# Loading two tiles ahead in the weight dequantisation of a two-layer macaron transformer

## The reference

```python
# layer 0
x = x + 0.5 * L0_ffn(layernorm(x))        # ternary weights, 1024 -> 4096 -> 1024
x = x + L0_attn(layernorm(x))             # linear attention, then an FFN with GELU inside it
x = x + 0.5 * L0_ffn(layernorm(x))
# layer 1
x = x + 0.5 * L1_ffn(x)                   # int weights, used twice
x = x + L1_attn(x)                        # softmax attention, 16 heads of 64
x = x + 0.5 * L1_ffn(x)

def _dequant(q, scales, g):               # q: int32 0..255, g = 128
    w = (q.astype(jnp.float32) - 128.0).reshape(K // g, g, N) * scales[:, None, :]
    return w.reshape(K, N)                # fc1: 1024 x 4096, fc2: 4096 x 1024
```

## Time and profile before

| | us |
|---|---|
| median of the runs (2) | 15,925.6 (15,891.4 to 15,959.7) |
| the profiled execution | 15,981.4 |
| its span on the slowest core (core 6) | 15,979.8 |
| spans of the 8 cores | 15,761.4 to 15,979.8 |
| TensorE busy | 9,455.1 (59%) |
| VectorE busy | 3,824.6 (24%) |
| ScalarE busy | 3,534.6 (22%) |
| GpSimd busy | 417.6 (3%) |

### The profile page before, as it was taken

How to read it: one execution, slowest core, us unless ns; L and a number is a source line. 1 busy time by engine, 2 the same in 40 slices (tenths; PEclk the granted TensorE clock), 3 DMA queues, 4 the chain that set the end, 5 groups by cost and what they waited for, 6 DMA issues and landing times.

```text
span 15979.8 us, 134598 instructions; the slowest of 8 cores (15761.4 to 15979.8 us)
## 1 busy us (share of the span) xinstructions
PE 9455.1 (59%) x37062; PEld 4058.4 (25%) x37544; DVE 3824.6 (24%) x7679; ACT 3534.6 (22%) x6356; POOL 417.6 (3%) x781
## 2 busy tenths in 40 slices
PE   0018884233333566553088878874777767677877
PEld 0003332111111344442033333332111111112333
DVE  0111214332233211111012123222322222223232
ACT  0323332100000111111033322221322413133221
POOL 0000000000000000001200000000000000000000
PEclk9998886655555677887599988875565565666999
DMA  9423332111111444543233323321000010101334
GB/s 149 128 75 95 99 99 61 64 51 47 52 49 46 121 140 140 141 138 114 61 99 101 108 89 97 100 86 49 16 31 31 16 37 16 37 24 38 108 101 138
DMA packets 683346, 1275.90 MB, mean 80 GB/s; under 512 B 60673, under 2 KB 200321, under 8 KB 679554
## 3 DMA queue, kind: packets, MB, share of 16 engines
q1 hardware_dynamic: 648690, 1149.75, 24.4%
q0 software_dynamic: 33936, 117.49, 3.6%
HBM read 1199.89 MB, written 134.22 MB: 83 GB/s over the span
## 4 chain that ended last, share of the span: by engine, by line
PE 42%; DMA 19%; DVE 18%; issue 9%; ACT 7%; another core or an unknown queue 2%; DVEq 1%; POOL 1%; SPq 0%; ACTq 0%; POOLq 0%
PE pb L790 12%; PE pb L863 7%; PE pb L1459 3%; PE pb L1422 3%; DMA ar_urng<-s_w 3%; DMA ar_drng<-s_w 3%; DVE ar_zbs L1471 3%; DMA ar_qi<-fc_p 2%; DMA ar_x2t<-s_x 2%; DMA ar_urng<-s_fc 2%; PE pb L1395 2%; PE pb L1490 2%; DVE ar_zq L1202 1%; PE pb L1170 1%
## 5 line engine op out<-in xcount | busy, mean ns | idle before, releaser
L790 PE MATMUL pb<-ar_x2t,ar_urng 128*128 128x512 bf16 (+1 forms) x12124 | 2612.2, 371 | 739.1 <-DMA ar_urng<-s_w 413.3
L863 PE MATMUL pb<-ar_ht,ar_drng 128*128 128x512 bf16 (+1 forms) x12072 | 2578.1, 370 | 406.8 <-DMA ar_drng<-s_w 256.8
L790 PEld LDWEIGHTS pb<-ar_x2t,ar_urng 128*128 128x128 bf16 x12288 | 1218.8, 105 | 2002.4 <-issue 1339.6
L863 PEld LDWEIGHTS pb<-ar_ht,ar_drng 128*128 128x128 bf16 x12288 | 1245.0, 105 | 1690.6 <-issue 1051.0
L1437 ACT ACTIVATE ar_pt<-pb,cpoolT 128x512 bf16<-128x512 f32 (+3 forms) x1408 | 1054.2, 749 | 2304.5 <-PE pb L1422 2276.7
L1459 PE MATMUL pb<-ar_pt,ar_vb 128*65 128x512 bf16 (+3 forms) x1408 | 815.0, 579 | 236.6 <-ACT ar_pt L1437 139.0
L800 ACT ACTIVATE ar_ht<-pb,vecsT 128x256 bf16<-128x256 f32 (+1 forms) x1024 | 594.7, 581 | 1239.5 <-PE pb L790 1236.6
L572 PE MATMUL bbk<-identbT,ar_lnT 128*128 128x128 bf16 x1792 | 199.8, 280 | 1001.8 <-DVE ar_lnT L556 420.3
L495 PE MATMUL pb<-identfT,xres 128*128 128x128 f32 x1536 | 295.0, 361 | 829.8 <-DMA s_fc<-ar_qo 506.9
L1422 PE MATMUL pb<-ar_qb,ar_ktb 64*128 64x512 bf16 (+3 forms) x1408 | 772.3, 567 | 17.6 <-DVE ar_qb L1357 17.6
L501 ACT ACTIVATE ar_trash<-pb 128x512 f32<-128x512 f32 x448 | 267.5, 597 | 1516.4 <-PE pb L495 1439.5
(11 more groups left out here) (139 smaller groups left out, 8095.8 us busy)
## 6 DMA issues: line engine op xcount, KB each, us to landing
ar_urng<-s_wup SPq DMA_DIRECT2D x256, 512.0 KB, 3.7
ar_drng<-s_wdn SPq DMA_DIRECT2D x512, 256.0 KB, 3.4
ar_urng<-s_w SPq DMA_DIRECT2D x256, 512.0 KB, 4.1
ar_drng<-s_w SPq DMA_DIRECT2D x512, 256.0 KB, 3.7
ar_urng<-s_fc SPq DMA_DIRECT2D x256, 512.0 KB, 3.8
ar_drng<-s_fc SPq DMA_DIRECT2D x512, 256.0 KB, 3.5
ar_x2t<-s_x SPq DMA_DIRECT2D x64, 1024.0 KB, 5.4
ar_ti<-wup_p SPq DMA_DIRECT2D x64, 512.0 KB, 3.9
```

Source lines behind the costliest of these rows:

```text
L790: e.matmul(pb[bank][:, 0:TT], urng[:, slot * 2048 + (f % 2) * D + k * 128: slot * 2048 + (f % 2) * D + (k + 1) * 128], x2t[:, half * XW + ...
L863: p.ins("tensor", lambda e, slot=slot, f=f, ff_=ff_, bank=bank: e.matmul(pb[bank][:, 0:TT], drng[:, slot * 1024 + f * 128: slot * 1024 + ( ...
```

## The change

`_deq` is split into `issue(i)`, which emits the two loads of tile i, and `compute(i)`, which emits its copy, multiply and store. The loads run two tiles ahead: two are issued at the start, and each step emits `compute(i)` and then `issue(i + 2)`. The wait for the buffer of `qi` to be free moves from SP's stream to GpSimd's, the engine that issues the load. At the start of each generator VectorE, ScalarE and GpSimd wait for the DMAs of `dqg` still in flight. Tiles, buffers, instructions and the number of DMAs stay as they were.

```diff
         tiles = [(oc, hf) for oc in range(OC) for hf in range(nh)]
-        otoks = []
-        cpyA = []
-        mulV = []
-        for i, (oc, hf) in enumerate(tiles):
+        n = len(tiles)
+        otoks = {}
+        cpyA = {}
+        mulV = {}
+        qtok = {}
+        stok = {}
+
+        def issue(i):
+            oc, hf = tiles[i]
             buf = i % NB
             pr = i % 2
             if i >= NB:
-                p.wait("sync", p.evA, cpyA[i - NB])
-            tkq = self.dqg.dma(lambda e, oc=oc, hf=hf, buf=buf: e.dma_start(
+                p.wait("gpsimd", p.evA, cpyA[i - NB])
+            qtok[i] = self.dqg.dma(lambda e, oc=oc, hf=hf, buf=buf: e.dma_start(
                 out=qi[:, buf * HIC:(buf + 1) * HIC],
                 in_=ap[qsrc][oc, :, hf * HIC:(hf + 1) * HIC]))
             if i >= 2:
                 p.wait("gpsimd", p.evV, mulV[i - 2])
-            tks = self.dqg.dma(lambda e, oc=oc, hf=hf, pr=pr: e.dma_start(
+            stok[i] = self.dqg.dma(lambda e, oc=oc, hf=hf, pr=pr: e.dma_start(
                 out=qs[:, pr * HIC:(pr + 1) * HIC],
                 in_=ap[ssrc][oc, :, hf * HIC:(hf + 1) * HIC]))
-            self.dqg.wait("scalar", tkq)
+
+        def compute(i):
+            oc, hf = tiles[i]
+            buf = i % NB
+            pr = i % 2
+            self.dqg.wait("scalar", qtok[i])
             if i >= 2:
                 p.wait("scalar", p.evV, mulV[i - 2])
...
-            self.dqg.wait("vector", tks)
+            self.dqg.wait("vector", stok[i])
             p.wait("vector", p.evA, p.evA.n)
             if i >= NB:
                 self.dqg.wait("vector", otoks[i - NB])
...
             p.wait("gpsimd", p.evV, p.evV.n)
-            otoks.append(self.dqg.dma(lambda e, oc=oc, hf=hf, buf=buf: e.dma_start(
+            otoks[i] = self.dqg.dma(lambda e, oc=oc, hf=hf, buf=buf: e.dma_start(
...
+
+        self.dqg.drain("vector")
+        self.dqg.drain("scalar")
+        self.dqg.drain("gpsimd")
+        issue(0)
+        if n > 1:
+            issue(1)
+        for i in range(n):
+            compute(i)
+            if i + 2 < n:
+                issue(i + 2)
             yield
```

More of the change, by code:

```diff
@@ L425, in _deq @@
         nh = IC // HIC
-        nb_banks = HIC // 512
         tiles = [(oc, hf) for oc in range(OC) for hf in range(nh)]
-        otoks = []
-        cpyA = []
-        mulV = []
-        for i, (oc, hf) in enumerate(tiles):
+        n = len(tiles)
[6 more added lines that the diff above has]
+            oc, hf = tiles[i]
             buf = i % NB
             pr = i % 2
-            spart = 32 if pr == 0 else 64
             if i >= NB:
-                p.wait("sync", p.evA, cpyA[i - NB])
-            tkq = self.dqg.dma(lambda e, oc=oc, hf=hf, buf=buf: e.dma_start(
+                p.wait("gpsimd", p.evA, cpyA[i - NB])
+            qtok[i] = self.dqg.dma(lambda e, oc=oc, hf=hf, buf=buf: e.dma_start(
                 out=qi[:, buf * HIC:(buf + 1) * HIC],
@@ L450, in _deq @@
                 ACTF.Copy, bias=-128.0))
-            cpyA.append(p.evA.n)
-            self.dqg.wait("vector", tks)
+            cpyA[i] = p.evA.n
+            self.dqg.wait("vector", stok[i])
             p.wait("vector", p.evA, p.evA.n)
@@ L459, in _deq @@
                 qs[:, pr * HIC:(pr + 1) * HIC]))
-            mulV.append(p.evV.n)
+            mulV[i] = p.evV.n
             p.wait("gpsimd", p.evV, p.evV.n)
-            otoks.append(self.dqg.dma(lambda e, oc=oc, hf=hf, buf=buf: e.dma_start(
+            otoks[i] = self.dqg.dma(lambda e, oc=oc, hf=hf, buf=buf: e.dma_start(
                 out=ap[dst][oc, :, hf * HIC:(hf + 1) * HIC],
-                in_=qo[:, buf * HIC:(buf + 1) * HIC])))
+                in_=qo[:, buf * HIC:(buf + 1) * HIC]))
+        self.dqg.drain("vector")
[8 more added lines that the diff above has]
+                issue(i + 2)
             yield
```

## The result

The changed kernel takes 15,412.5 us (median of 11 runs, 15,289 to 15,658); the kernel before, beside it, 15,945.9 us (median of 10). The ratio is 0.9632, 95% interval 0.9603 to 0.9661: 3.7% faster. In some runs the cores of one half of the chip show a lower granted clock than the others and take longer; the ratio leaves these runs out, and so is not the quotient of the two medians. The profiled execution has a span of 15,410.9 us on core 6.

The account below looks back on a forecast made before the run. The prediction took about 1,136 us of exposed dequantisation latency as the bound; savings of 251 (drain), 206 (attention) and 105 (FFN), 562 us together, gave a forecast median of 15,365 us, range 15,240 to 15,550.

Parts of the forecast that it names:

- The loop and its sharing: Dequantisation: the 4.94 us loop from multiply through store and loads to multiply now carries two tiles, 2.47 us each.
- The drain's term: 96 tiles alone between two fences: 2.62 us a tile in place of 5.23, saving 251 us (215 to 265).
- the four semaphores: GpSimd's DMA queue: each DMA waits for the one four earlier to land; 0.5 us to spare, binding above 3.0 us.
- loads at 3.5 us: Drain, low end: with four loads in flight, landing takes 3.5 us, a tile 3.0 us, saving 215 us.
- The attention's term: 16 blocks of 6 tiles in the linear attention: 160 us from 12 blocks plus 46 from four, 206 us saved.
- wait for `x2t` until 3561: Attention blocks opening a head group: `x2t` lands last, TensorE starts at 3561 instead of 3572.57, 11.6 us saved each.
- The FFN's term: 16 blocks of 4 tiles in the attention's FFN: 105 us saved of 134 us of long waits (50 to 134).
- The clock: FFN stage behind the drain: a shorter drain might lower its granted clock, at most 128 us; taken as 0.
- rival 3: Slower by the clock: less idle time drops the busy FFN stages to 1.2 GHz, 16,586 us; chance 0.02.
- The shared port: VectorE's multiply overlapping GpSimd's issues: between 0 and 0.42 us a tile lost on the loop; taken as 0.
- The price of 40 us: Drain: gain lost if VectorE and GpSimd lock their shared port pair, up to 96 x 0.42 us.
- One sign I named: ScalarE's idle time before the dequantisation's copy, 2092.6 us, was to fall well under half.

Follow-up runs that it names:

- e1: Kernel before with only the wait for the buffer of `qi` moved from SP to GpSimd; ratio 0.998 to the kernel before, drain 495 us.
- e4: Changed kernel with three tiles loaded ahead, three scales buffers and eight semaphores; ratio 0.952 to the kernel before, drain 191 us.
- e7: Changed kernel with the loads of tile i+2 issued ahead of the store of tile i; ratio 0.960 to the kernel before, drain 227 us.
- e2: Changed kernel with the wait for the buffer of `qi` put back on SP; ratio 0.973 to the kernel before, attention 2,095 us.
- e3: Changed kernel with eight semaphores for GpSimd's DMA queue in place of four; ratio 0.966 to the kernel before, drain 263 us.
- e5: Changed kernel without any dequantisation, stages 4 and 6 reading the bf16 weights of the attention's FFN; ratio 0.937 to the kernel before.

## Why the prediction was right, and where it was off

**The loop and its sharing** held in all three places, and e1 and e4 show it apart from its rivals; e7 rules out a throughput limit at 2.75 us. Two tiles of the changed kernel, in the drain:

```profile
7166.92 0.43 DVE L464 TENSOR_TENSOR ar_qo<-ar_qf,ar_qs 128x256 bf16<-128x256 f32 x1 [2.05 <-DMA ar_qs<-fc2s_p]
7167.96 0.55 POOL L470 DMA_DIRECT2D s_fc<-ar_qo  x1 [0.80 <-DVE ar_qo L464]
7168.52 0.54 POOL L440 DMA_DIRECT2D ar_qi<-fc_p  x1
...
7169.32 0.54 POOL L445 DMA_DIRECT2D ar_qs<-fc2s_p  x1 [0.26 <-issue]
7169.93 0.43 DVE L464 TENSOR_TENSOR ar_qo<-ar_qf,ar_qs 128x256 bf16<-128x256 f32 x1 [2.59 <-DMA ar_qs<-fc2s_p]
...
7172.10 0.54 POOL L445 DMA_DIRECT2D ar_qs<-fc2s_p  x1
7172.17 0.43 DVE L464 TENSOR_TENSOR ar_qo<-ar_qf,ar_qs 128x256 bf16<-128x256 f32 x1 [1.81 <-DMA ar_qs<-fc2s_p]
```

From the multiply at 7166.92 over its store and the loads to the next but one at 7172.17 is 5.25 us, with another multiply between. In the earlier trace rows the same way took 4.94 with none.

**The drain's term** was 251 and came out at 238: a tile takes 261.0 / 95 = 2.75 us (first store 7059.77, last 7320.79), not 2.62. The mis-sized part is the loop, which I had left at the 5.2 us of before. Taken apart, in means over the drains of the eight cores, before and after:

| from | to | before | after |
|---|---|---|---|
| multiply | store's issue | 1.07 | 1.12 |
| store's issue | issue of `qi` | 0.56 | 0.61 |
| issue of `qi` | issue of the scales | 0.59 | 0.74 |
| issue of the scales | multiply | 2.99 | 2.98 |
| the loop | | 5.21 | 5.44 |

All of the growth is on GpSimd's side of the loop, none in the landing: in the drain the load of `qi` lands 2.52 us after its issue before and 2.53 after (medians), at 63 and at 117 GB/s. So the fear that I gave the low end of the term for, loads at 3.5 us, did not come true. What grew: the issues are 0.57 apart instead of 0.54 (the first two in the rows above, 0.56); GpSimd pauses more often (0.26 above); and the scales' load waited for the ring 11 times in a drain, 9 us in all, where I had called the four semaphores just clear. The term was inside the range I gave it (215 to 265). The 0.57 comes with the moved wait and not with the overlap: e1, which only moves it and overlaps nothing, has 0.57 from store to load, and e2, which prefetches with the wait on SP, has 0.53.

**The attention's term** was 206, and the stage is 201 shorter; by TensorE's own wait it is 190. On this core the wait fell by 12.2 us in each of the 12 blocks (13.3 forecast) and by 10.9 in each of the four that open a head group (11.6 forecast). In the second block TensorE waited 28.05 us before:

```profile
3076.08 1.86 PE L1075 MATMUL pb<-ar_wkb,ar_x2t 128*128 128x512 bf16 x4 [28.05 <-DVE ar_qo L456]
```

It waits 17.64 now; timeline of the changed kernel, the last row at the head of the second head group:

```profile
2945.20 0.54 POOL L440 DMA_DIRECT2D ar_qi<-fc_p  x1 [3.57 <-DMA s_fc<-ar_qo]
...
2955.41 1.87 PE L1093 MATMUL pb<-ar_wkb,ar_x2t 128*128 128x512 bf16 x4 [17.64 <-DVE ar_qo L464]
...
3419.84 3.57 PE L1093 MATMUL pb<-ar_wkb,ar_x2t 128*128 128x512 bf16 x8 [24.51 <-DVE ar_qo L464]
```

The first row shows the step that failed in part. I had found the four semaphores "just clear", with the load of tile 3 behind a store issued over 5 us earlier. Stores land 1.9 us after their issue in the median, but at the head of a block this one is under way together with the 1 MB of `x2t` and took 5.3, and GpSimd stood 3.57 us. e3 shows that it costs nothing in sum. In the blocks that open a head group I had TensorE wait for `x2t` until 3561, saving 11.6 us; the last row shows it released by the multiply again, 24.51 us where the earlier trace rows had 34.46, 10.0 saved. The multiply is the releaser in all four such blocks. In this one `x2t` had landed 1.8 us earlier, so the two run close together. Nearly the right size, wrong releaser.

**The FFN's term** was 105, the stage is 96 shorter. TensorE stood 134 us at the heads for ScalarE and stands 14; but 14 first-weight waits, 11.4 to 13.2 us before (170.6 in sum), are 11.5 to 14.4 now (181.3), 0.8 us each where I had said 1, and the waits for `urng` rose from 413.3 to 438.4. In the medians of the eight cores TensorE's waits for ScalarE fell by 118 us and those for the weights rose by 44 (`urng` 37, `drng` 7), which leaves 74 of the 96 explained. The weight feed took back 44 where I had allowed 29 (134 less 105); the other 22 us I cannot assign. They are not the clock: e1, with the old loop and the same granted clock in this stage (0.845), takes 2,172 us. This one is the softest of the three: the stage's median was 2,051 to 2,074 in five kernels with the prefetch.

**The clock** gave and took nothing behind the drain: 0.91 on this core, stage 3 at 1,325 us beside 1,329, although the drain's idle time was halved. e5 goes further: it has no drain at all, and its stage 3 takes 1,325 us at a granted clock of 0.93 in the median of the cores, which is 0.93 in the kernels before and after too. So the idle drain was not what let stage 3 have its clock, and rival 3 had nothing to stand on.

**The shared port.** VectorE's multiply does overlap GpSimd's issue now, at 7172.10 and 7172.17 above, and both keep their durations, 0.54 and 0.43; over all 256 the multiply stays at 424 to 427 ns and the store's issue at 542 to 545. Over the eight cores 1,094 of the 2,048 multiplies overlap an issue of GpSimd, where before none did, and they take 424 to 427 ns like the others. The price of 40 us that I had worked out beside the Trainium skill's page SBUF — State Buffer (section "Who interferes with whom") was not paid. The Trainium skill has, on the same page in section "SBUF: two separate sides", VectorE instructions with two SBUF inputs contend only with a GpSimd operation that reads SBUF. The durations agree with that if issuing a DMA is not such a read, which no run here shows apart; I had read the page too widely.

**One sign I named was wrong.** ScalarE's idle time before the copy was to fall well under half of 2,092.6 us; it fell to 1,496.0 only, as the page of the changed kernel has it among its groups:

```profile
L456 ACT ACTIVATE ar_qf<-ar_qi 128x256 f32<-128x256 int32 x256 | 106.5, 416 | 1593.3 <-DMA ar_qi<-fc_p 1496.0
```

and ScalarE's timeline around one head of a token tile:

```profile
6253.30 0.92 ACT L456 ACTIVATE ar_qf<-ar_qi 128x256 f32<-128x256 int32 x2
6304.85 0.42 ACT L456 ACTIVATE ar_qf<-ar_qi 128x256 f32<-128x256 int32 x1 [50.63 <-DMA ar_qi<-fc_p]
```

The timeline shows why: the two copies whose loads were prefetched run early, and then ScalarE has nothing to do for 50 us until the block itself comes. All of that is put down to the load that ended it. The waits of TensorE fell as forecast, and they were the ones to watch.

**The size in all:** 562 us forecast, 535 in the three stages; 15,365 us forecast for the median, 15,412.5 measured. All three terms came out 5 to 13 us under the forecast, so no error hid another. The ratio gives 587 us, 52 more than the stages; the stages behind them are 17 us longer in sum in the profiled execution, so no stage shows where the 52 us come from.

## What to carry to other kernels

A side job of small load, compute and store steps on an in-order queue costs its loop, not its work: find the loop in one period of the timeline, and divide it by the number of tiles that can be under way; one, two and three gave 5.23, 2.75 and 1.95 us here, the last near the 1.70 us in which the queue issues three DMAs. Before running further ahead, ask where the steps stand: one step at a time, put between TensorE's instructions and the wait for them, was worth more (0.945, and 3,979 us in the three stages) than a third tile in flight (0.952, and 4,243 us), and with it the third tile was worth nothing. And a wait that a block hid comes back when the block goes: of 1,136 us waited for the side job, 1,003 were to be had. Last, once the loop is short, ask again what releases the queue: with the loads ahead of the store (e7) it was no longer the multiply but the ring of four semaphores.

## What the runs showed of the hardware

- In the drain, where the core moves nothing else, loads of 128 KB issued by GpSimd land 2.52 us after their issue at 63 GB/s, 2.53 at 117 and 2.75 at 166 (medians of the loads of `qi` over the eight cores of the kernel before, the changed one and e4; bandwidth of one core): overlapping them up to this rate costs little.
- Beside the weight loads of the inner FFN the same load takes 3.5 us before, 4.2 in the changed kernel and 4.9 in e4 (medians likewise; 137 and 145 GB/s in the first two): there, further ahead means slower from issue to landing.
- GpSimd issues a DMA every 0.54 us in the kernel before and every 0.57 in the changed one and in e1, which has one wait more in GpSimd's stream, although each issue is busy 0.54 to 0.55 in all of them.
- A VectorE multiply of two SBUF operands that overlaps a DMA issue of GpSimd takes 424 to 427 ns, as without an overlap (1,094 of 2,048), and the issue keeps its 0.54 us.
- Halving 505 us of TensorE's idleness left the granted clock of the stage behind it at 0.91 (0.92 before, core 6), and taking it away altogether (e5) at 0.93 (0.93 before and 0.93 in the changed kernel, medians of the cores).
